# State space pipeline: the spread rows of B go through an SBUF copy by ACT, and spreads are issued a step sooner

## The reference, cut to what matters

```python
xz = x @ W_in
xc, z = jnp.split(xz, 2, axis=-1)
xs = silu(causal_conv(xc, conv_w) + conv_b)          # 4 taps
A = -jnp.exp(A_log)                                  # 256 channels x 16 states
x_dbl = xs @ W_x
d_raw, Bp, Cp = x_dbl[..., :1], x_dbl[..., 1:17], x_dbl[..., 17:]
delta = softplus(d_raw * w_dt + b_dt)
def step(h, inp):                                    # over the 512 tokens
    dt, b, c, xt = inp
    h = jnp.exp(dt[..., None] * A) * h + (dt * xt)[..., None] * b[:, None, :]
    return h, jnp.einsum('bdn,bn->bd', h, c)
y = (scan(step) + xs * D) * silu(z)
return y @ W_out
```

## Time and profile before

| | us |
|---|---|
| median of 3 runs | 3414.5 (3413.73 to 3419.38) |
| the profiled execution | 3416.19 |
| span of the core in it | 3414.4 |
| busy in the span: PE, DVE, ACT, POOL | 2524.0, 2234.6, 1497.3, 1138.9 |
| state space stage, steps only | from about 1751 to 2445 |

### The profile page before, as it was taken

The page is one execution under the profiler, slowest core; times in us unless marked ns, Lnnn a source line. Parts: engine busy times, 40 slices in busy tenths (PEclk is TensorE's granted clock), DMA queues, the critical chain, the costliest instruction groups (busy, mean ns, idle before and its releaser), DMA issues. The chain is left out here.

```text
span 3414.4 us, 49243 instructions
## 1 busy us (share of the span) xinstructions
PE 2524.0 (74%) x17446; PEld 1269.1 (37%) x17454; DVE 2234.6 (65%) x4562; ACT 1497.3 (44%) x2911; POOL 1138.9 (33%) x1172
## 2 busy tenths in 40 slices
PE   3999987874898876775557777677624846899986
PEld 1333334442444445554522222222214842233334
DVE  4888868784667644342368887888742237888854
ACT  1777761110555542222344444444311214777751
POOL 3222104432221202232435555555573433222001
PEclk9999997775899986556877877777856976999989
DMA  5111100000211201005800000000014942212100
GB/s 161 32 39 28 31 1 0 1 0 19 42 31 38 45 25 39 14 19 169 255 9 1 0 0 0 0 0 1 0 35 158 292 145 43 48 30 41 20 4 22
DMA packets 129156, 157.01 MB, mean 46 GB/s; under 512 B 18000, under 2 KB 110288, under 8 KB 128304
## 3 DMA queue, kind: packets, MB, share of 16 engines
q1 hardware_dynamic: 119248, 139.91, 15.7%
q0 software_dynamic: 6592, 13.56, 1.1%
q10 hardware_dynamic: 3072, 0.40, 0.1%
HBM read 95.56 MB, written 25.59 MB: 35 GB/s over the span
## 5 line engine op out<-in xcount | busy, mean ns | idle before, releaser
L422 DVE TENSOR_REDUCE a_mx<-banks 128x1 f32<-128x512 f32 (+3 forms) x1536 | 882.6, 618 | 253.3 <-PE banks L762 123.1
L633 ACT ACTIVATE a_prob<-banks 128x512 f32<-128x512 f32 (+3 forms) x1536 | 773.9, 545 | 382.4 <-PE banks L785 156.9
L785 PE MATMUL banks<-a_Qs,a_Ks 64*128 64x512 bf16 (+3 forms) x1536 | 512.6, 368 | 48.1 <-ACT a_prob L633 40.9
L762 PE MATMUL banks<-a_Ks,a_Qs 63*128 63x512 bf16 (+3 forms) x1536 | 503.1, 375 | 45.7 <-DVE a_mx L422 32.7
L813 PE MATMUL banks<-a_prob,a_vaug 128*32 128x256 f32 (+2 forms) x5632 | 446.3, 390 | 0.7 <-ACT a_prob L633 0.5
L2073 PE MATMUL banks<-m_hc,kc 128*128 128x512 f32 x512 | 340.5, 765 | 118.5 <-POOL m_hc L1949 99.5
L1949 POOL TENSOR_TENSOR m_hc<-m_h,m_cs 128x512 f32<-128x512 f32 x256 | 327.9, 1297 | 287.0 <-DVE m_h L1813 274.7
L1996 ACT ACTIVATE banks<-m_dt,acoef 128x512 f32<-128x512 f32 x256 | 175.8, 691 | 297.2 <-DVE m_h L1813 296.9
L1813 DVE TENSOR_TENSOR_SCAN m_h<-banks,m_u 128x512 f32<-128x512 f32 x256 | 301.6, 1209 | 0.0
L762 PEld LDWEIGHTS banks<-a_Ks,a_Qs 63*128 63x128 bf16 x1536 | 126.7, 95 | 406.0 <-DVE a_mx L422 220.7
L1798 DVE TENSOR_TENSOR m_u<-m_dtx,banks 128x1024 f32<-128x1024 f32 x128 | 155.3, 1213 | 104.6 <-PE banks L2054 102.0
(11 more groups left out here) (405 smaller groups left out, 4730.3 us busy)
## 6 DMA issues: line engine op xcount, KB each, us to landing
c_wbuf<-in_w2e SPq DMA_DIRECT2D x71, 512.0 KB, 4.2
b_wbuf<-in_w1e SPq DMA_DIRECT2D x39, 578.0 KB, 4.4
a_Ks<-a_parts SPq DMA_DIRECT2D x288, 64.0 KB
a_Qs<-a_parts SPq DMA_DIRECT2D x288, 64.0 KB
rows_in<-in_unused SPq DMA_DIRECT2D x1, 4579.5 KB, 16.7
c_yb<-rows_in SPq DMA_DIRECT2D x71, 64.5 KB, 4.8
a_mixed_in<-rows_back SPq DMA_DIRECT2D x16, 256.0 KB, 3.9
a_Qs<-a_negm ACTq DMA_DIRECT2D x192, 2.0 KB
```

The source lines that it names most:

```text
L422: dve.tensor_reduce(mx[:, g % 2, col:col + 1], M[:, k % 3, 0:keys[j]], AX.X, ALU.max).then_inc(S("max_read"), 1)
L633: act.activation(prob[:, n % 8, first_query[kt]:T], Sc[:, n % 2, first_query[kt]:T], ACT.Exp, scale=scale).then_inc(S("exped"), 1)
L762: i = pe.matmul(M[:, k % 3, 0:keys[j]], Qs[lo:lo + LAST, b % 4, pair, j * P:(j + 1) * P], Ks[lo:lo + LAST, b % 4, pair, 0:keys[j]], start= ...
L785: i = pe.matmul(Sc[:, n % 2, q0:T], Ks[lo:lo + HALF, b % 4, pair, kt * P:(kt + 1) * P], Qs[lo:lo + HALF, b % 4, pair, q0:T], start=True, s ...
```

## The change

The spread rows of B get an SBUF buffer `bs` with four places. ACT copies `Bs` into it (a new instruction for each of 128 steps, signalling `b_taken`), and DVE's product reads `bs` instead of the PSUM bank. The matmul that overwrites `Bs` waits for that copy and no longer for the product. The copy waits for the product of four steps back. The due times move: the spread from -3.4 to -6.6, the C copy from -2.8 to -5.3; the B copy is at -5.5. So ACT's order becomes decay(k-1, 0), B copy(k), C copy(k), decay(k-1, 1), decay(k, 0), and on PE spread(k) stands before the sums of step k-3, where it stood after them. Product, decays, scans, `hc` and sums keep their due times.

```diff
-                cs, yf = room("cs", [P, 4, T]), room("yf", [P, NCH, T])
+                bs, cs, yf = room("bs", [P, 4, T]), room("cs", [P, 4, T]), room("yf", [P, NCH, T])
...
-                        dve.wait_ge(S("b_spread"), k + 1)
+                        dve.wait_ge(S("b_taken"), k + 1)
...
-                        dve.tensor_tensor(u[:, k % 3], dtx[:, b % 2], Bs.unsqueeze(1).broadcast_to([P, NCH, T]),
+                        dve.tensor_tensor(u[:, k % 3], dtx[:, b % 2], bs[:, k % 4, :].unsqueeze(1).broadcast_to([P, NCH, T]),
...
-                        yield at(k) - 2.8
+                        yield at(k) - 5.5
+                        act.wait_ge(S("b_spread"), k + 1)
+                        if k >= 4:
+                            act.wait_ge(S("u_ready"), k - 3)
+                        act.activation(bs[:, k % 4, :], Bs, ACT.Copy).then_inc(S("b_taken"), 1)
+                        yield at(k) - 5.3
                         act.wait_ge(S("c_spread"), k + 1)
...
                         if k:
-                            pe.wait_ge(S("u_ready"), k)
+                            pe.wait_ge(S("b_taken"), k)
...
-                        yield at(k) - 3.4
+                        yield at(k) - 6.6
                         spread(k)
```

## The result

The changed kernel takes **3477.7 us** (median of 4 runs, 3468.09 to 3480.06), the kernel before 3415.35 us in the same comparison (4 runs, 3413.73 to 3419.38): ratio 1.0175, 95% interval 1.0154 to 1.0197, +62 us. It is slower, by under 2%, and the time lies 2.7 us above the upper end of the predicted range. The profiled execution took 3468.09 us.

What follows compares the result with a forecast made beforehand. VectorE's order was taken to set the time, the late spread of B being the only wait to win (ceiling 102 us). Gains and losses summed to +4.7 us on the 3414.5 us median, giving 3420 us, range 3400 to 3475.

Steps and rivals of the forecast that it cites:

- The spread one step sooner: Prediction's working of the earlier B spread: product waits for ACT's copy behind one decay, starting 2.49 us after the first scan's start.
- 27 steps with TensorE full: State space steps where TensorE is busy throughout: pitch falls from 3.87 to 3.62 us, -6.8 us in all.
- free-running ones: 17 state space steps where nothing waits, most in the last batch: pitch 3.36 becomes 3.62 us, +4.4 us in all.
- the sum: All slips and gains traced through one middle batch's four queues and added up: +4.7 us.
- steps 1 to 4: Early steps of each batch: sooner products, but GpSimd's small operation and gate are held up, sum 0.0 for each batch.
- first steps of four batches: Four batch starts: spread no longer behind sums waiting for GpSimd's backlog, 4 x -1.23 = -4.9 us.
- SiLU: Steps around ACT's table switches: copies delay the switch and the copy to G, 7 x 0.97 = +6.8 us.
- The port race: SBUF port in each free-running step: product comes 0.03 us ahead of GpSimd's second `hc` and wins.
- Rival (a): GpSimd's second `hc` takes the SBUF port first in each step: step 4.78 us, kernel 3471 us, chance 0.22.
- Turnover: Change of batch: the product after the G part finds `hc` in the port, 7 x 0.96 = +6.7 us.
- The copy's cost on VectorE: Product's own duration when it reads SBUF instead of PSUM: about 1.20 us either way, taken as nothing.
- Rival (b): The spread's gain holds, gate delay hidden and copies fitting ACT's waits at SiLU: -20 us, 3400 us, chance 0.16.

## Why the prediction was wrong, step by step

- **The step that failed** is in "The spread one step sooner": "this copy stands behind the first decay of step k-1". It stands behind both. The working from there (decay at +1.25, 0.63, 0.58, 0.03) has the right durations and the wrong decay: with the second one the product starts at 2.33 + 1.27 = 3.60 after the first scan's start instead of 2.49, and 3.60 + 1.18 = 4.78 is the pitch. The 27 steps with TensorE full cost +0.92 instead of -0.25 each, 32 us beside the forecast; the free-running ones +1.42 instead of +0.26, 17 x 1.16 = 20 us. That is 51 of the 58 us between 3420 and 3478. The order could have been read from the code: one generator, whose pieces keep the order of its text.
- **The rest of the sum held in total, less so in its terms.** With the order that it assumed the kernel takes 3420.56 us against 3420 (+2.9 on its own kernel before, where the sum says +4.7), and the pitch is 3.63 against 3.62, in free-running and TensorE-full steps. That the total meets so closely is partly luck. In that kernel steps 1 to 4 of the six middle batches cost 4.0 us (forecast 0.0), the first steps of four batches gain 8.9 (forecast 4.9), and SiLU costs 3.5 (forecast 6.8): at full clock it would be 8.3 (13.01 became 14.20, seven times), but the kernel before loses 5.0 us there by its slower projections, of which the prediction says nothing.
- **The port race** was priced as worked out, and won. Rival (a) gives the pitch of 4.78 that is measured, and 3471 us, but for another reason: it asks for a product of over 2.3 us behind the second `hc`. The rows show a product of 1.26 that had waited 1.27 for ACT. That two mechanisms lead to one figure is chance; the duration of the product and the releaser of the wait tell them apart, the pitch does not.
- **Turnover**: forecast +0.96 each. In three batches +2.0 is measured (3.69 to 5.70), of which 0.96 is the port (4.74 without it), as worked out, and the other half is the second decay. In the other four it is +1.29 (7.47 to 8.76), of which 0.46 is the port (8.30 without it).
- **Steps 1 to 4**: forecast 0.0; measured +0.3 summed over eight batches (+8.25 - 7.96), but that is +5.4 in the first and last and -5.1 in the six between, for which the 0.0 was meant. Nor is it as described: the product found the gate already running (product 2.34, gate 2.35), where the forecast had it the other way round.
- **SiLU**: forecast 14.0 to 15.0, measured 13.98 to 15.13 in the second batch. With the order assumed it is 14.2 (8.26 + 5.94), so here too the agreement is not the forecast's mechanism. Both 13.98 and 15.13 hold projections at the lower clock; where it is full, 13.01 became 13.62. (The forecast's parts, 0.54 - 0.58 + 1.1, give 1.06 and not 0.97.)
- **First step of four batches**: forecast -1.23 each; 6.05 became 4.99, -1.06 (-0.85 in one).
- **The copy's cost on VectorE**: taken at nothing, and right: 1.22 from PSUM against 1.23 from SBUF where the port is free.
- **Rival (b)** undervalued what the spread was worth. Its 3400 us kept the copy; the spread alone gives 3368. The prediction never priced that part by itself, and so did not see that the copy costs 110 us against the simpler edit. The chance of slower (0.48) was the largest, but the range ended at 3475 because both of its upper cases started from the same assumed order.

## What to carry to other kernels

Where pieces are sorted by due times, a due time works only from the moment at which its generator offers the piece: read ACT's real order from the rows or the generators before a wait is priced, and never from the numbers alone. A copy that releases a buffer sooner puts its engine between producer and consumer; ask which instruction it stands behind, and for whom that one waits, since here a ring of scan, decay, copy and product cost 57 us against the same copy one decay sooner, a copy of 0.58 us a step. Try the sooner issue alone before the copy is added: here it held the whole gain.

## What the runs showed of the hardware that was not expected

- VectorE's product with two SBUF inputs, coming 0.03 us ahead of GpSimd's `hc`, gets its way (1.23 us long, the `hc` 2.32), and is blocked in the one step of the last batch in which it comes 0.03 behind (2.32 long). The Trainium skill, SBUF — State Buffer, section "Who interferes with whom", says that the shared port pair is an exclusive lock and that issue order decides who blocks; the rows agree (2.18 and 2.34 beside an `hc` and the gate that had begun 0.61 and 1.08 us earlier).
- The blocked instruction is recorded from its issue and not from its true start: the product of 1.26 starts 0.18 before the `hc` ahead of it ends and is only 0.04 longer than 1.22, so all but some 0.14 of such an overlap is waited out.
- Where the copy is there in time, product and `hc` pairs settle into a steady 3.56 us per step instead of 3.36, the product recorded with 1.39, the first `hc` with 1.27 and the second with 2.25. Over the stage reading the copy costs 27 us.
- The clock that TensorE is granted differs between profiled executions of nearly the same kernel: four projection matmuls take 3.49 us in one batch (clock 0.63 over the stretch) and 1.99 in another (1.00), in five of seven batches of the changed kernel and in none with the copy between the decays. A difference of some microseconds between such kernels is read with the granted clock beside it.
